# Cross-attention and mixture of experts on one core: token weights by transfers instead of a spreading product, and another order in the prelude

## The reference

```
x = x + attention(layernorm(x), ctx, ctx, mask)      # 16 heads of 8, keys and values from ctx
x = x + moe(layernorm(x))

moe(t): logits = t @ router_w.T                      # 16 experts
        two best of (logits + router_bias), softmax over these two scores -> two weights per token
        out = sum over the 16 experts of weight * (silu(t @ gate_e) * (t @ up_e)) @ down_e
              + (silu(t @ sh_gate.T) * (t @ sh_up.T)) @ sh_down.T          # shared expert, weight 1
```

## Time and profile before

| | us |
|---|---|
| median of 3 runs | 202.36 |
| the profiled execution | 201.04 |
| its span | 199.2 |
| TensorE busy | 181.9 (91%) |
| VectorE busy | 162.8 (82%) |
| ScalarE busy | 128.5 (64%) |
| GpSimd busy | 90.1 (45%) |
| mean granted TensorE clock | 0.974 of full speed |

### The profile page before, as it was taken

One profiled execution on the slowest core, in us unless ns is written; L12 is line 12 of the kernel. 1 busy time (PEld: TensorE's weight loads), 2 busy tenths in 40 slices (PEclk: granted clock), 3 DMA queues, 4 the chain that ended last, 5 costly groups with the idle time before them and its releaser, 6 DMA issues.

```text
span 199.2 us, 4347 instructions
## 1 busy us (share of the span) xinstructions
PE 181.9 (91%) x1351; PEld 128.8 (65%) x1351; DVE 162.8 (82%) x510; ACT 128.5 (64%) x290; POOL 90.1 (45%) x152
## 2 busy tenths in 40 slices
PE   8889581799999999999989899999999999999973
PEld 8665341467666666666666577777777777777742
DVE  5679957379999989999999799967977798778881
ACT  2298087189999989999968664564555544555531
POOL 7057937758888888888767741500000000000000
PEclk9999967599999999999999999999999999999999
DMA  5999100000000000000000000000100010001001
GB/s 122 301 327 390 64 0 0 2 3 0 2 3 5 0 0 0 0 0 5 0 0 5 0 0 3 0 0 0 53 2 2 0 53 0 0 0 53 0 3 53
DMA packets 7008, 7.21 MB, mean 36 GB/s; under 512 B 848, under 2 KB 5456, under 8 KB 6864
## 3 DMA queue, kind: packets, MB, share of 16 engines
q1 hardware_dynamic: 5680, 5.56, 8.9%
q10 hardware_dynamic: 1312, 1.46, 2.6%
HBM read 5.97 MB, written 1.05 MB: 35 GB/s over the span
## 4 chain that ended last, share of the span: by engine, by line
PE 67%; DVE 15%; POOL 6%; issue 5%; DMA 4%; ACTq 1%; ACT 1%; DVEq 0%; POOLq 0%
PE bank L1084 35%; PE bank L1036 11%; PE bank L1018 5%; PE bank L1027 4%; DMA mhalf<-mask_half 4%; PE bank L1124 3%; POOL k_blk L457 2%; POOL rstd L431 2%; DVE prob L847 2%; PE bank L1007 2%; DVE smax L826 2%; PE bank L997 2%; PE bank L987 1%; DVE k_all L761 1%; PE bank L992 1%
## 5 line engine op out<-in xcount | busy, mean ns | idle before, releaser
L641 ACT ACTIVATE sig<-bank 128x512 f32<-128x512 f32 x36 | 21.5, 599 | 33.6 <-PE bank L1084 33.3
L1036 PE MATMUL bank<-k_blk,q_blk 128*128 128x512 f32 x64 | 36.1, 649 | 6.8 <-POOL k_blk L457 4.2
L457 POOL TENSOR_TENSOR k_blk<-k_all,consts_sb 128x512 f32<-128x512 f32 x32 | 32.7, 1044 | 0.0
L887 DVE TENSOR_TENSOR hid_u<-sig,bank 128x512 f32<-128x512 f32 x32 | 22.0, 686 | 11.5 <-PE bank L1084 8.8
L1084 PE MATMUL bank<-xt_hi,w_hi 128*128 (+1 forms) x72 | 29.4, 408 | 0.0
L598 ACT ACTIVATE prob<-prob,exp_scale 128x512 f32<-128x512 f32 x32 | 23.8, 743 | 7.4 <-DVE prob L847 6.3
L1084 PE MATMUL bank<-xt_hi,w_lo 128*128 (+1 forms) x72 | 28.1, 390 | 0.0
L1084 PE MATMUL bank<-xt_lo,w_hi 128*128 (+1 forms) x72 | 28.1, 390 | 0.0
L826 DVE TENSOR_REDUCE smax<-bank 128x8 f32<-128x512 f32 x32 | 22.0, 686 | 5.6 <-PE bank L1036 5.5
L896 DVE TENSOR_TENSOR hid_lo<-hid,hid_hi 128x512 fp32r<-128x512 f32 (+1 forms) x37 | 25.2, 683 | 0.6 <-ACT hid_hi L650 0.5
L650 ACT CAST hid_hi<-hid 128x512 fp32r<-128x512 f32 (+1 forms) x37 | 22.2, 603 | 2.5 <-DVE hid L903 2.3
(11 more groups left out here) (126 smaller groups left out, 358.8 us busy)
## 6 DMA issues: line engine op xcount, KB each, us to landing
w_moe_sb<-w_moe SPq DMA_DIRECT2D x1, 1296.0 KB, 8.5
ctxt_sb<-ctx_t SPq DMA_DIRECT2D x4, 256.0 KB, 8.5
xt_sb<-x_t ACTq DMA_DIRECT2D x4, 256.0 KB, 8.1
x_sb<-x SPq DMA_DIRECT2D x4, 256.0 KB, 10.7
out<-x_sb SPq DMA_DIRECT2D x3, 256.0 KB, 2.3
w_moe_sb<-w_moe SPq DMA_DIRECT2D x1, 432.0 KB, 8.0
w_att_sb<-w_att SPq DMA_DIRECT2D x1, 264.0 KB, 3.8
sel_sb<-expert_sel SPq DMA_DIRECT2D x1, 256.0 KB, 8.2
```

Of the source, the lines that this page charges most:

```text
L457: last = nc.gpsimd.tensor_tensor(k_blk[p][:, g, :, :], k_all[:, bass.ds(t, 1), g, :].broadcast_to([P, HG, S]), hmask_sb.rearrange("p (h o) ...
L641: nc.scalar.activation(sig[r][:, :], gate_ps[r][:, :], ACT.Silu).then_inc(s_sig, 1)
L887: nc.vector.tensor_tensor(dst[:, :], sig[r][:, :], up_ps[r][:, :], ALU.mult).then_inc(s_hid_u, 1)
L1036: nc.tensor.matmul(score_ps[g][:, :], q_blk[q][:, g, :, :].rearrange("p b s -> p (b s)"), k_blk[q][:, g, :, :].rearrange("p h s -> p (h s) ...
```

## The change

In the prelude VectorE now does step -1 right behind the keys and statistics of group 0, and one further group of both behind the scores of steps -1, 0 and 1. TensorE and ScalarE do step -1 before the keys of group 2, GpSimd masks groups 2 and 3 behind the blocks of tile 0, and its waits and inverse roots stand in steps 0 to 3. ScalarE's queue loads the first columns of x_t before the mask row.

The token weights are laid out by expert first, [128 tokens, 16 experts, 8 tiles], which is a square for half of the tokens. One fp32 transpose turns it, ScalarE copies it to SBUF, and SP stores it to a buffer in DRAM. From there 32 transfers on the SP queue, one for each group and pair of experts, read two rows of 512 weights, each repeated 64 times, into one of four SBUF buffers `cb`. The weighted product reads `cb`. The three parts, `sel_sb`, the bf16 identity, the spreading products and `up`'s wait for hid go.

The buffers, and SP:

```diff
-        comb_t = sb("comb_t", [P, TOKENS], BF16)
+        comb_row = [sb(f"comb_row{h}", [P, P]) for h in range(2)]
+        cb = [sb(f"cb{k}", [P, GN]) for k in range(CB_BUFS)]
+        comb_dram = nc.dram_tensor("comb_rows", (2, EXPERTS, TOKENS // 2), F32, kind="Internal").ap()
...
-            sp.dma_start(sel_sb[:, :, :], expert_sel).then_inc(s_wmoe[1], 16)
-            sp.dma_start(identb_sb[:, :], ident_bf).then_inc(s_wmoe[1], 16)
-
-            for n in range(GROUPS - 1 + 2):
+
+            def result_out(n):
                 sp.wait_ge(s_y, n + 1)
...
+            def weights_out(half):
+                sp.wait_ge(s_ct_sb, half + 1)
+                sp.dma_start(comb_dram[half].rearrange("e (t n) -> (e t) n", n=P), comb_row[half][:, :])\
+                    .then_inc(s_comb_out[half], 16)
+                sp.wait_ge(s_comb_out[half], 16)
+
+            def weights_of_pair(g, pair):
+
+                n = g * EPAIRS + pair
+                if n >= CB_BUFS:
+                    sp.wait_ge(s_hid, n - CB_BUFS + 1)
+                cols = slice(g % 2 * GN, (g % 2 + 1) * GN)
+                rows = comb_dram[g // 2, 2 * pair:2 * pair + 2, cols].rearrange("e (o n) -> e o n", o=1)
+                sp.dma_start(cb[n % CB_BUFS][:, :], rows.broadcast_to([2, E_DIM, GN])).then_inc(s_cb[n % CB_BUFS], 16)
+
+            for g in range(GROUPS):
+                if g % 2 == 0:
+                    weights_out(g // 2)
+                for pair in range(EPAIRS):
+                    weights_of_pair(g, pair)
+                    if pair == EPAIRS - 2 and g > 0:
+                        result_out(g - 1)
+            for h in range(2):
+                result_out(GROUPS - 1 + h)
```

On GpSimd:

```diff
             mask_ctx(1)
-            mask_ctx(2)
...
             k_blocks(0, 0)
+            mask_ctx(2)
+            rstd1_of(0)
             mask_ctx(3)
-            rstd1_of(0)
             q_block(1, 1, first=True)
             k_blocks(1, 1)
-            for g in range(1, GROUPS):
-                rstd1_of(g)
-            nc.gpsimd.memset(comb_t[:, :].bitcast(F32), 0.0).then_inc(s_comb_zero, 1)
-            pool.wait_ge(s_q_sb, GROUPS)
-            pool.wait_ge(s_k_sb, GROUPS)
...
+                if isinstance(t, int) and t <= TRAIL:
+                    groups = GROUPS if t == TRAIL else (t + 2) // GT + 1
+                    pool.wait_ge(s_q_sb, groups)
+                    pool.wait_ge(s_k_sb, groups)
...
                     k_blocks(t + 2, p)
+                    if isinstance(t, int) and t < GROUPS - 1:
+                        rstd1_of(t + 1)
...
-            expert_weights(pool, nc.gpsimd, 1, s_route[1])
+            combined(pool, nc.gpsimd, 1, s_route[1])
```

On ScalarE:

```diff
+                if isinstance(t, int) and t == TILES - 1:
+                    weights_to_sbuf(0)
...
+            def weights_to_sbuf(half):
+                act.wait_ge(s_ct, half + 1)
+                nc.scalar.copy(comb_row[half][:, :], ct_ps).then_inc(s_ct_sb, 1)
...
             for g in range(GROUPS):
-                if g == GROUPS - 1:
+                queries_out(g)
+                if g == GROUPS - 2:
                     peel(step, LEAD)
-                project(g)
+                keys_out(g)
+                if g == 0:
+                    shares()
+                values_out(g)
```

On VectorE:

```diff
+                if isinstance(t, int) and t == LEAD:
+                    keys(1)
+                    norm1(1, 1)
+                if isinstance(t, int) and 0 <= t < GROUPS - 2:
+                    keys(t + 2)
+                    norm1(t + 2, t % 2)
                 if isinstance(t, int) and t == TILES - 4:
                     experts_marked(0)
+                    weights_of_two(0)
                 if isinstance(t, int) and t == TILES - 3:
-                    weights_of_two(0)
-                if isinstance(t, int) and t == TILES - 2:
                     combined(dve, nc.vector, 0, s_route[0])
-                if isinstance(t, int) and t == TILES - 1:
-                    in_parts(dve, nc.vector, 0, s_route[0], range(PARTS))
...
                 dve.wait_ge(s_hid_u, n + 1)
-                dve.wait_ge(s_cb, g * EPAIRS + m)
-                nc.vector.tensor_tensor(hid[m % 3][:, :], hid_u[r][:, :], cb_ps[r][:, :], ALU.mult).then_inc(s_hid, 1)
+                k = (m - 1) % CB_BUFS
+                dve.wait_ge(s_cb[k], 16 * (g * (EPAIRS // CB_BUFS) + (m - 1) // CB_BUFS + 1))
+                nc.vector.tensor_tensor(hid[m % 3][:, :], hid_u[r][:, :], cb[k][:, :], ALU.mult).then_inc(s_hid, 1)
```

On TensorE:

```diff
             for g in range(GROUPS):
-                if g == GROUPS - 1:
+                queries(g)
+                if g == GROUPS - 2:
                     peel(step, LEAD)
-                project(g)
+                keys_values(g)
...
                 else:
                     pe.wait_ge(s_sub[0], TILES)
                     gate(0, 0)
+                    weights_as_rows(0)
...
+                pe.wait_ge(s_route[half], 2)
+                nc.tensor.transpose(ct_ps, comb[half][:, :, :].rearrange("p e t -> p (e t)"), ident_sb).then_inc(s_ct, 1)
...
-                if m >= 3:
-                    wait_hid(pe, g, m - 2)
-                elif m > 0 and not isinstance(g, int):
-                    wait_hid(pe, g, m - 3)
...
-            def token_weights(g, m):
-                pe.wait_ge(s_ct_sb, min(m, 2) if isinstance(g, int) else 4)
-                nc.tensor.matmul(cb_ps[m % 2][:, :], sel_sb[:, m - 1, :], comb_t[:, bass.ds(g * GN, GN)], start=True,
-                                 stop=True).then_inc(s_cb, 1)
```

More of the change, by code:

```diff
@@ L54, with build_program @@
 W_FIRST = 4 * W_STEP
+CB_BUFS = 4
 SCORE_SCALE = float(DK) ** 0.5
-def build_program(nc, x, x_t, ctx_t, mask_row, mask_half, mask_col, w_att, router_bias, w_moe, consts, ident_bf,
-                  expert_sel, out):
+def build_program(nc, x, x_t, ctx_t, mask_row, mask_half, mask_col, w_att, router_bias, w_moe, consts, out):
     stack = ExitStack()
@@ L148, in build_program @@
         w_top = sb("w_top", [P, TILES, 2])
-        comb = sb("comb", [P, TILES, EXPERTS])
-        comb_b = sb("comb_b", [P, TILES, EXPERTS])
-        comb3 = sb("comb3", [P, TILES // 2, PARTS, EXPERTS], BF16)
+        comb = [sb(f"comb{h}", [P, EXPERTS, TILES // 2]) for h in range(2)]
+        comb_b = [sb(f"comb_b{h}", [P, EXPERTS, TILES // 2]) for h in range(2)]
         sig = [sb(f"sig{p}", [P, GN]) for p in range(2)]
@@ L251, in build_program @@
         s_up = sem("s_up")
-        s_cb = sem("s_cb")
+        s_comb_out = [sem(f"s_comb_out{h}") for h in range(2)]
+        s_cb = [sem(f"s_cb{k}") for k in range(CB_BUFS)]
         s_sig = sem("s_sig")
@@ L280, in build_program @@
         up_ps = [banks[6], banks[0]]
-        cb_ps = banks[1:3]
+        ct_ps = banks[2][:, 2 * P:3 * P]
         moe_ps = banks[3]
@@ L352, in wait_hid @@
                 eng.wait_ge(s_hid, g * EPAIRS + (m + 1))
-        def expert_weights(eng, ops, half, written):
-            combined(eng, ops, half, written)
-            in_parts(eng, ops, half, written, range(PARTS))
         def combined(eng, ops, half, written):
             tiles = slice(half * TILES // 2, (half + 1) * TILES // 2)
-            shape = [P, TILES // 2, EXPERTS]
             eng.wait_ge(s_w_top, half + 1)
-            for k, dst in ((0, comb), (1, comb_b)):
-                last = ops.tensor_tensor(dst[:, tiles, :], dst[:, tiles, :], w_top[:, tiles, k:k + 1].broadcast_to(shape),
-                                         ALU.mult)
+            for k, dst in ((0, comb[half]), (1, comb_b[half])):
+                last = ops.tensor_tensor(dst[:, :, :], dst[:, :, :],
+                                         w_top[:, tiles, k].rearrange("p (o t) -> p o t", o=1)
+                                         .broadcast_to([P, EXPERTS, TILES // 2]), ALU.mult)
             last.then_inc(written, 1)
             eng.wait_ge(written, 1)
[L368 to L384, removed]
+            ops.tensor_tensor(comb[half][:, :, :], comb[half][:, :, :], comb_b[half][:, :, :], ALU.add).then_inc(written, 1)
         def w_slice(w, u, kind):
@@ L547, in shares, with queries_out @@
                         .then_inc(s_vden, 1)
[L549 removed]
+            def queries_out(g):
                 act.wait_ge(s_q, g + 1)
@@ L556, in project, with values_out @@
                                k_ps[g % 2][:, :].rearrange("p (g t s) -> p g t s", g=2, t=GT)).then_inc(s_k_raw, 1)
-                if g == 0:
-                    shares()
+            def values_out(g):
                 act.wait_ge(s_v, g + 1)
@@ L772, in experts_marked @@
                 tiles = slice(half * TILES // 2, (half + 1) * TILES // 2)
-                shape = [P, TILES // 2, EXPERTS]
-                iota_bc = iota_sb.rearrange("p (o e) -> p o e", o=1).broadcast_to(shape)
+                shape = [P, EXPERTS, TILES // 2]
+                iota_bc = iota_sb.rearrange("p (e o) -> p e o", o=1).broadcast_to(shape)
                 dve.wait_ge(s_top_f, (half + 1) * TILES // 2)
```

(20 more changed lines are left out.)

43 lines of the change are left out of this document (6 added, 37 removed).

## The result

| kernel | median us | runs | ratio to before (95%) |
|---|---|---|---|
| before, beside it on the chip | 202.25 (201.69 to 202.51) | 4 | |
| changed | 283.64 (283.04 to 284.31) | 4 | 1.403 (1.398 to 1.408) |

What follows compares the result with a forecast made beforehand. Spread transfers on two DMA engines were taken to bound the expert stage. First spread at 99.5, plus 1.4, 176.0 (32 x 5.5), 2.0 and 2.8, gives 281.7; 6.8 and 0.7 make span 289.2, with 1.84 outside 291.0 us; range 272 to 313.

Steps and rivals of the forecast that it cites:

- the pace: Expert stage: each pair's factor transfer on two engines takes 5.5 us, bounds 5.04 and 6.04.
- first spread issued: End of attention: gate 0 at 96.0, rows store issued by 97.6, landed some 1.9 us later, first spread issued at 99.5.
- from there to the first weighted product: Start of the expert stage: a transfer's fixed part, 1.4 us, then one pair's data, 5.5 us.
- dry line, and three stores of results: Expert stage: SP's line runs dry between groups 1 and 2, 2.0 us; three result stores on the same engines, 2.8 us.
- behind it, to the end of the span: Tail after the last factor: 6.8 us as before the change, plus 0.7 for TensorE work at a lower clock.
- The prelude: Start of the kernel: the new order brings step 4 to 45.5 against 51.04, 5.5 us gained, bounds 2 to 8.
- plus 0.3 for the moved VectorE work: End of attention, before gate 0 of step 15: marks and products one step earlier cost 0.3 us.
- The stall behind the wait: Expert stage: VectorE's weighted product waits 3 us and more each for its transfer; issue to landing near 20 us.
- TensorE's share: Sign over the whole kernel: TensorE's busy share falls under 70%.
- the DMA share: Sign in the expert stage: near 0.12 without a gap from about 98 us to the end.
- The fast rival: Expert stage: spreads on 16 engines land in 2.3 us, hidden; TensorE bounds, 13.1 us gained, median 189.2; chance 0.14.
- The third rival: Expert stage: two engines, each slowed to the small packets' 17.4 GB/s, 7.5 us per pair, 355 us; chance 0.02.

Runs made afterwards that it cites:

- the prelude alone: The kernel before with only the prelude's new order on all five engines, token weights as before: 197.15 us, 0.978 of before.
- the kernel with four engines: The changed kernel with token weights stored twice in DRAM, so each pair's transfer reads [4 rows, 32 repeats, 512]: 202.47 us, 1.004 of before.
- the kernel with two transfers: The changed kernel with each pair's factor loaded by two transfers of 64 partitions, one row repeated 64 times each: 190.66 us, 0.947 of before.

## Why the prediction was right

It said 291.0 with 272 to 313, and 284.31 was the profiled execution, 283.64 the median. The mechanism, the place of the wait and the count of packets were as said. The error is one term's size, with a smaller one against it: 11.5 us too much for the pace, and 4.8 too little in the other steps. That the total is off by only 6.7 is in part luck. By the steps of its sum, each to the row that answers it:

| step | predicted | measured | difference |
|---|---|---|---|
| first spread issued | 99.5 | 103.04 | +3.5 |
| from there to the first weighted product | 6.9 (1.4 + 5.5) | 7.7 | +0.8 |
| 31 paces | 170.5 | 159.0 (31 x 5.13) | -11.5 |
| dry line, and three stores of results | 2.0 + 2.8 | 2.1 + 2.9 | +0.2 |
| last factor | 281.7 | 274.75 | -7.0 |
| behind it, to the end of the span | 7.5 | 7.75 | +0.2 |
| outside the span | 1.8 | 1.8 | 0 |

**The pace** was the mis-sized term: "a straight line through 29.4 ns for 512 B and 399 ns for 10,368 B gives 87 ns for 2 KB". The runs show 5.13 us for 64 packets, 80 ns each, 25.5 GB/s for an engine against 26.0 in the densest row. It lies by the lower bound (5.04). The straight line treats each packet as a fixed part and a rate, but the 2 KB packets cost nearly what their bytes do at the rate of the 10 KB ones. The 512 B row was the one far off. It was also a row of a store, where the other row and the spreads are loads; which of the two, size or direction, makes it slower is not shown.

**The prelude** had the second error. These are TensorE's scores of tiles 2 to 5 and gate 0 of step 15 in the changed kernel:

```profile
28.60 1.12 PE L1033 MATMUL bank<-k_blk,q_blk 128*128 128x512 f32 x2
...
34.98 1.12 PE L1033 MATMUL bank<-k_blk,q_blk 128*128 128x512 f32 x2
...
43.30 1.10 PE L1033 MATMUL bank<-k_blk,q_blk 128*128 128x512 f32 x2
...
47.77 1.12 PE L1033 MATMUL bank<-k_blk,q_blk 128*128 128x512 f32 x2
...
99.13 0.48 PE L1086 MATMUL bank<-xt_hi,w_hi 128*128 128x512 f32 x1
```

Tile 2 came at 28.60 for a forecast 28.0, and step 1 took 6.4 us, inside the 6 to 7. Step 2 took 8.3 (34.98 to 43.30), where 6 to 7 stood, and tile 5 came at 47.77, for 50.90 in the same view of before: 3.1 us gained, not 5.5. The changed kernel's chain has the keys of groups 2 and 3 on VectorE in both of these steps:

```profile
29.92 0.73 DVE k_all L758
...
35.85 0.75 DVE k_all L758
```

Group 3's start ahead of step 2's row maximum (38.89 on that chain), and the scores of tile 4 wait for both. But this is not all of the 8.3. The prelude alone and the kernel with four engines have the same order, and there tile 4 comes at 42.14 and 42.11, 6.8 and 7.1 us after tile 3. What differs is TensorE's clock. These are the same 3 us of the changed kernel and of the one with four engines:

```profile
40.00:43.00 3.00, 2.97 (x41) 2.58 (x41) 2.15 (x4) 2.20 (x6) 2.92 (x4) 0.50 0.00 0
```

```profile
40.00:43.00 3.00, 2.96 (x44) 2.18 (x45) 2.77 (x15) 2.82 (x8) 2.92 (x4) 1.00 0.00 0
```

In both TensorE had done nothing from 38 to 40 us; why its clock fell to the lower level in one of them is open. At full clock tile 5 comes at 47.3, 5.2 us after tile 4 where the forecast had 4.5: there GpSimd's inverse root (41.90 in the prelude alone) stands on the chain between two steps. So of the 2.4 us by which the prelude fell short of 5.5, some 1.9 lie in the order itself, spread over steps -1 to 3, and 0.5 came with the clock. The 4.4 us of the prelude alone lie between the bounds of 2 and 8, and 1.1 under the 5.5. A further 0.8 us came at the end of attention: the step "plus 0.3 for the moved VectorE work" was too small. From the scores of tile 14 to those of tile 15, and from there to gate 0, the changed kernel takes 5.32 and 5.10 us (88.71, 94.03, 99.13), the prelude alone 4.76 and 4.53 (88.27, 93.03, 97.56): 1.1 us for marks and products one step earlier, 0.8 more than taken. The rows store landed in 2.5, not 1.9, and the three products, transpose and copy ahead of it took 1.4 and not 1.6. So the first spread was late by 2.4 + 0.75 + 0.6 - 0.2 = 3.55.

**The stall behind the wait** went as said: VectorE's largest wait is the weighted product's, near 3 us each, and a spread landed 18.87 us after its issue, "near 20". The dry line (2.1 for 2.0) and the stores of results (0.75, 0.75 and 1.4 more than the pace, for 3 x 0.94) held within 0.1 in sum; why the last store cost twice as much as the others is open.

**One sign missed, one was off.** TensorE's share is 72%, not under 70%. It does less work (1305 products for 1351) in 21 us more of busy time, because the granted clock is 0.80 on average from 103 to 275 us (the same 1305 products take 172.7 us in the kernel with two transfers, at 0.99): the engine idles in each pair, and parts of the stage ran at the lower of the two levels (1.2 GHz, 0.50 in the stretch from 190 to 191), where its products take longer. It costs nothing here, since the transfers bind; the forecast had counted the clock only in the tail, 0.7 us. And the DMA share is 0.14 over the stage for a forecast 0.12 without a gap: the stage has a gap, from 188 to 190, but a faster pace and the stores of results in it.

**The fast rival** had 189.2 us. Given its engines, the kernel takes 190.66, 6.5 under the prelude alone where its terms summed to 7.65 (0.8 + 1.4 + 0.45 + 5.5 - 0.5). Its group of 9 x 2.13 = 19.13 us is what its terms say (20.88 before, less 8 x 0.23, so 19.05); the last group is slower, as the loop of 2.05 us shows itself there. Of its 13.1 us of gain 10.9 came (201.52 less 190.66): 1.1 is missing from the prelude and 1.15 from the rest. The third rival's 17.4 GB/s is refuted by 25.5. The prediction gave two engines 0.82 on packet counts and one rule. The rule of the Trainium skill ("DMA: Bandwidth & Descriptors", section "Why a DMA increments its semaphore by 16 and not by 1") says that the engines are the largest number up to 16 which divides the outermost dimension (sizes of 1 not counted) of both sides. The packet counts agree with it at four values: 2, 4, 8 and 16 engines by 9840, 10192, 10896 and 10288 packets, each count forecast before its run. The pace bears out two of them, 5.13 us for 2 and 2.57 for 4. All these dimensions are powers of two, so no run here tells "divides" from "at most".

## What to carry to other kernels

Before a transfer is put in a loop, look at the outermost dimension of both its sides: [2, 64 repeats, 512] and [64 repeats, 2, 512] move the same bytes to the same number of partitions. Here the first took 5.13 us each, one behind the other, and the second landed in 3.1 us, hidden behind TensorE, and that was 92 us of 284. The profile page of one run tells how many engines a shape got: take a queue's packets, subtract the data packets by their shapes and 16 for each transfer of the usual shape, and divide the rest by the number of the new transfers. And to see whether transfers will bind, compare pace with slot (bytes per engine over the 25.5 GB/s measured, against 2.1 us here). Where they bind, more buffers lengthen the line: four in place of two changed nothing.

## What the runs showed of the hardware

A store on all engines suffers from a narrow line ahead of it in two ways. Its issue held SP for 4.97 us, about one spread's time, where a store's issue takes 0.37 at the end of the same kernel, and it landed 14.4 us after issue at the median (2.3 before, 3.0 with spreads of 64 partitions); the 64 KB of rows took SP 3.69 us to issue. The two are separate: with two buffers the store's issue took 0.47 to 0.54 us, and it still landed 9.8 us after issue. The hold came with the third and fourth spread in line on two engines, 192 and 256 data packets for each engine. With two in line on two engines, or four in line on four (0.51 us for a spread's issue at the median, 0.43 for a result's), each has up to 128, and the longest issues were 1.6 and 2.2 us, of stores of rows. What fills up was not tried.

The clock followed the stalls, though not by a fixed amount: 0.91 from 110 to 120 us and 0.67 from 120 to 130, at the same pace of 5.13 us, with TensorE busy 6.5 and 6.6 of the 10 us.
